# Nine more input chunks held in the first pass's space ahead of a two-layer convolution, and 15 warm-up matmuls in place of 7

## The reference

```
x = x + _L0_conv_ref(_gn(x), L0_conv_w_fft_real, L0_conv_w_fft_imag, ...)
x = x + _L1_conv_ref(_gn(x), L1_conv_weight)
```

## Time and profile before

| | |
|---|---|
| median of 3 runs | 1762.68 us (1761.88 to 1762.94) |
| the profiled execution | 1762.14 us, of which the span is 1760.3 us |
| TensorE matmuls busy | 1653.9 us (94%) |
| VectorE busy | 1381.3 us (78%) |
| ScalarE busy | 1169.0 us (66%) |
| GpSimd busy | 130.9 us (7%) |
| mean granted clock of TensorE | 0.98 |

### The profile page before, as it was taken

One profiled execution on the slowest core, in us unless ns is written; L12 is line 12 of the kernel. 1 busy time (PEld: TensorE's weight loads), 2 busy tenths in 40 slices (PEclk: granted clock), 3 DMA queues, 4 the chain that ended last, 5 costly groups with the idle time before them and its releaser, 6 DMA issues.

```text
span 1760.3 us, 65152 instructions
## 1 busy us (share of the span) xinstructions
PE 1653.9 (94%) x29295; PEld 1263.6 (72%) x29295; DVE 1381.3 (78%) x2202; ACT 1169.0 (66%) x1050; POOL 130.9 (7%) x383
## 2 busy tenths in 40 slices
PE   5888888688799999999999999999999999999999
PEld 5888878554466667887788668866886678666755
DVE  5998999789988888888887888788878888878600
ACT  6888788579666666666666666666666666666444
POOL 0000000032200020002000200020002000100100
PEclk9999899889899999999999999999999999999999
DMA  9999999565456666656665666666666665666245
GB/s 385 421 421 422 422 421 421 210 187 163 121 162 206 199 194 213 216 188 202 214 206 195 202 218 195 205 196 212 196 203 208 202 209 194 209 196 207 110 197 205
DMA packets 101979, 411.65 MB, mean 234 GB/s; under 512 B 17139, under 2 KB 19688, under 8 KB 85352
## 3 DMA queue, kind: packets, MB, share of 16 engines
q1 hardware_dynamic: 100329, 407.51, 65.9%
q10 hardware_dynamic: 735, 0.37, 0.1%
q0 software_dynamic: 672, 0.08, 0.1%
HBM read 271.83 MB, written 136.07 MB: 232 GB/s over the span
## 4 chain that ended last, share of the span: by engine, by line
PE 69%; DVE 16%; issue 8%; ACT 3%; DMA 2%; DVEq 0%; POOL 0%; SPq 0%; ACTq 0%; POOLq 0%
PE ps L459 36%; PE ps L452 32%; DVE x L737 9%; DVE x L957 2%; DVE nat L798 2%; ACT x L578 1%; DVE stats L995 1%; DMA x<-x_pix 1%; ACT x L576 1%; ACT nat L563 1%; DMA x<-wf 1%; PE ps L387 1%; DMA xin<-x_tiles 0%; PE ps L388 0%; DVE x L798 0%
## 5 line engine op out<-in xcount | busy, mean ns | idle before, releaser
L459 PE MATMUL ps<-x,wc 64*64 64x512 f16 (+2 forms) x12585 | 1159.7, 374 | 6.0 <-POOL x L715 6.0
L452 PE MATMUL ps<-nat,wc 64*64 64x512 f16 (+1 forms) x11784 | 1137.6, 377 | 15.3 <-DVE x L957 11.3
L459 PEld LDWEIGHTS ps<-x,wc 64*64 64x64 f16 x12585 | 677.6, 107 | 178.4 <-POOL x L715 7.1
L452 PEld LDWEIGHTS ps<-nat,wc 64*64 64x64 f16 x11784 | 655.9, 107 | 190.2 <-issue 33.3
L563 ACT ACTIVATE nat<-xin,gnp 128x1024 f16<-128x1024 f32 (+1 forms) x249 | 283.3, 1138 | 295.8 <-PE ps L452 284.5
L957 DVE SCALAR_TENSOR_TENSOR x<-ps,gnp,x 128x1024 f16<-128x1024 f32 (+1 forms) x264 | 333.1, 1262 | 31.2 <-ACT x L578 21.6
L593 ACT ACTIVATE outb<-ps,bias 128x1024 f32<-128x1024 f32 (+1 forms) x264 | 289.7, 1097 | 73.1 <-PE ps L459 57.5
L582 ACT ACTIVATE x<-ps,gnp 128x1024 f16<-128x1024 f32 (+1 forms) x229 | 251.0, 1096 | 118.7 <-DVE stats L995 118.4
L798 DVE SCALAR_TENSOR_TENSOR nat<-xin,gnp,nat 128x1024 f16<-128x1024 f32 (+1 forms) x249 | 313.4, 1259 | 2.0 <-ACT nat L563 1.9
L387 PE MATMUL ps<-x 128*128 128x129 f16 x2048 | 259.9, 227 | 54.2 <-DVE x L737 54.0
L737 DVE SCALAR_TENSOR_TENSOR x<-x 128x2048 bf16<-128x2048 f32 x128 | 282.8, 2287 | 19.1 <-DMA x<-wf 17.3
(11 more groups left out here) (139 smaller groups left out, 384.2 us busy)
## 6 DMA issues: line engine op xcount, KB each, us to landing
x<-x_pix SPq DMA_DIRECT2D x128, 1024.0 KB, 11.2
xin<-x_tiles SPq DMA_DIRECT2D x256, 512.0 KB, 3.8
out<-outb SPq DMA_DIRECT2D x256, 512.0 KB, 4.1
xin<-x_tiles SPq DMA_DIRECT2D x8, 192.5 KB, 2.4
out<-outb SPq DMA_DIRECT2D x8, 192.5 KB, 3.0
w<-taps_scratch SPq DMA_DIRECT2D x60, 8.0 KB, 2.9
w<-taps_scratch SPq DMA_DIRECT2D x30, 16.0 KB, 3.2
taps_scratch<-x POOLq DMA_DIRECT2D x21, 3.0 KB, 3.0
```

Of the source, the lines that this page charges most:

```text
L452: return nc.tensor.matmul(ps[64 * kind:64 * kind + 64, bank, 0:w], lhs, planes[rows, xhl, a:a + w], start=first, stop=last)
L459: ins = nc.tensor.matmul(ps[64 * kind:64 * kind + 64, bank, done:done + part], lhs, x1[rows, xhl, z:z + part], start=first and done == 0, ...
```

## The change

Chunks 4 to 12 (`STAGED`) are loaded into `big`, where the first pass had its input, once that pass has read it. They have semaphores of their own. The natural halves of chunks 7 to 12 lie in slots 25 to 30 of `x1`, so 13 chunks have their place at once. The cycle over seven places begins again at chunk 13 (`LAP`), and the change to four places comes at chunk 34 (`TURN`) and not 35. GpSimd makes all pads of image 0, from the scaling factors on (`Z_GNP`); chunks 0 to 12, the join at 4, chunks 13 to 16 and the join at 7 stand ahead of the transfers of the taps of images 1 to 7. ScalarE makes `hi0(0)` between two square roots of the small chain, 1 to 3 ahead of its weight transfers and 4 to 9 behind; in the turns it is ten chunks ahead up to turn 6, makes none in turns 7 to 9 and is seven ahead from turn 10. VectorE makes `lo0(0)` inside the small chain, 1 to 4 ahead of the weights and 5 and 6 behind; in the turns it is seven ahead, as before. 15 warm-up matmuls stand in place of 7.

```diff
-TURN = (NCH // NSEVEN + 1) * NSEVEN
+STAGED = range(NX, NX + 9)
+LAP = STAGED.stop
+TURN = LAP + 3 * NSEVEN
+HI_FIRST = 10
+SIX_AT, STAGE_AT = 25, 6
-WARM = 7
+WARM = 15
+def ahead_hi(g):
+    if g + HI_FIRST < LAP + NX:
+        return g + HI_FIRST
+    return ahead(g) if g + NSEVEN >= LAP + NX else None
...
 def nat_at(g):
-            spot = g % NSEVEN if g < TURN else (g - TURN) % NX
+            if NSEVEN <= g < LAP:
+                return x1, (SIX_AT + g - NSEVEN) * CH
+            spot = g if g < LAP else (g - LAP) % NSEVEN if g < TURN else (g - TURN) % NX
...
+        def x_at(g):
+            if g in STAGED:
+                a = (STAGE_AT + 2 * (g - NX)) * CH // 2
+                return big[:, a:a + CH]
+            return xin[:, g % NX, :]
...
 SyncE:
-                if g >= NX:
-                    sp.wait_ge(lo0_ready, g - NX + 1)
+                if g >= LAP:
+                    sp.wait_ge(lo0_ready, (g % NX if g < LAP + NX else g - NX) + 1)
...
                 sp.dma_start(dst, src).then_inc(late_in, 16)
+            sp.wait_ge(a_lo, B * NACH + ASLOTS)
+            for g in STAGED:
+                load_x(g)
             hold(sp, zve, Z_ZPAD)
...
-            for g in range(NX, 2 * NX):
+            for g in range(LAP, LAP + NX):
                 load_x(g)
...
-                if g + 2 * NX < ALL:
+                if LAP + NX <= g + NSEVEN + NX < TURN + NX:
+                    load_x(g + NSEVEN + NX)
+                if TURN + NX <= g + 2 * NX < ALL:
                     load_x(g + 2 * NX)
...
 ScalarE:
             nc.scalar.activation(zc[0:C, 48:64], zc[0:C, 32:48], ACT.Sqrt).then_inc(zac, 1)
+            hi0(0)
             act.wait_ge(zve, Z_BNVAR)
...
-            for g in range(2):
+            for g in range(1, NX):
                 hi0(g)
             act.wait_ge(zdma, 16 * 4)
             load_weights(act, 0, ((0, 1), (1, 1)), w_in)
-            for g in range(2, NX):
-                hi0(g)
-            for g in range(NX, NSEVEN):
+            for g in range(NX, HI_FIRST):
                 hi0(g)
...
-                if ahead(g) is not None:
-                    hi0(ahead(g))
+                if ahead_hi(g) is not None:
+                    hi0(ahead_hi(g))
...
 GpSimd:
-            pool.wait_ge(zve, Z_TAPS)
-            pool.wait_ge(zdma, 16 * 4)
-            for b in range(1, B):
-                taps_out(pool, b, taps_rest)
+            pool.wait_ge(zve, Z_GNP)
+            for g in range(LAP):
+                first_pad(g)
+            join(NX)
+            for g in range(LAP, LAP + NX):
+                first_pad(g)
+            join(NSEVEN)
+            pool.wait_ge(zve, Z_TAPS)
+            pool.wait_ge(zdma, 16 * 4)
+            for b in range(1, B):
+                taps_out(pool, b, taps_rest)
...
 VectorE:
+            lo0(0)
             after_act(3)
...
-            for g in range(NX):
-                pad(g)
             after_pe()
...
-            for g in range(2):
+            for g in range(1, NX + 1):
                 lo0(g)
             for part in range(4):
                 weights0(0, part)
-            for g in range(2, NX):
+            for g in range(NX + 1, NSEVEN):
                 lo0(g)
-            for g in range(NX, NSEVEN):
-                pad(g)
-            for g in range(NX, NSEVEN):
-                lo0(g)
-            pad(NSEVEN)
```

More of the change, by code:

```diff
@@ L216, in conv_program @@
         x_in = [sem(f"x_in{s}") for s in range(NX)]
+        x_early = [sem(f"x_early{g}") for g in STAGED]
         w_in = sem("w_in")
@@ L534, in _, with hi0 @@
                                              ACT.Identity, scale=AS).then_inc(a_hi, 1)
+            def hi0(g):
+                b, n = divmod(g, NCH)
+                w = CH if n < NFULL else EDGE
+                if g < NCH:
+                    act.wait_ge(pool_pad, g + 1)
+                else:
+                    act.wait_ge(pad_done, g + 1 - NCH)
+                if g >= LAP:
+                    act.wait_ge(pe_done, JOB0[g - (LAP if g < LAP + NSEVEN else NSEVEN if g < TURN + NX else NX)] + 1)
+                planes, a = nat_at(g)
+                nc.scalar.activation(planes[:, 0, a:a + w], x_at(g)[:, 0:w], ACT.Identity,
+                                     scale=gnp[:, 1, b:b + 1]).then_inc(hi0_ready, 1)
             act.wait_ge(zve, Z_VAR)
             nc.scalar.activation(zc[0:C, 48:64], zc[0:C, 32:48], ACT.Sqrt).then_inc(zac, 1)
+            hi0(0)
             act.wait_ge(zve, Z_BNVAR)
@@ L549, in _ @@
                                      bias=trig[:, 2 * k + 1:2 * k + 2], scale=trig[:, 2 * k:2 * k + 1]).then_inc(zac, 1)
[L551 to L564, removed]
             def hi1(g):
@@ L658, in row_ends @@
                     done += w
-            pool.wait_ge(zve, Z_TAPS)
-            pool.wait_ge(zdma, 16 * 4)
-            for b in range(1, B):
-                taps_out(pool, b, taps_rest)
             def first_pad(g):
                 mean = gnp[:, 0, 0:1]
-                slot = xin[:, g % NX, :]
-                pool.wait_ge(x_in[g % NX], 16 * (g // NX + 1))
+                slot = x_at(g)
+                x_landed(pool, g)
                 lo, rows = ROWS_CH * g, ROWS_CH
+                if g == 0:
+                    G.tensor_copy(slot[:, 0:PITCH], mean.to_broadcast([P, PITCH]))
+                    lo, rows = PITCH, ROWS_CH - 1
                 if g == NFULL:
@@ L688, in ends @@
                 column_ends(b, (last + 1) * CH // PITCH if last else 0, TROWS if n == NFULL else (n + 1) * CH // PITCH)
+            pool.wait_ge(zve, Z_GNP)
[9 more added lines that the diff above has]
+                taps_out(pool, b, taps_rest)
             for turn in range(NCH):
-                if DVE_FIRST <= turn + 9 < NCH:
+                if LAP + NX <= turn + 9 < NCH:
                     first_pad(turn + 9)
-                if joins(turn + NSEVEN - 1):
+                if turn + NSEVEN - 1 > NSEVEN and joins(turn + NSEVEN - 1):
                     join(turn + NSEVEN - 1)
```

32 lines of the change are left out of this document (22 added, 10 removed).

## The result

The changed kernel takes 1757.49 us (median of 8 runs, 1755.63 to 1758.74) against 1762.45 us before (8 runs beside them): a ratio of 0.9971, 95% interval 0.9961 to 0.9981. That is 5.0 us or 0.3% faster, by the interval 3.3 to 6.9 us. 1756.2 was forecast with a range of 1753.8 to 1760.3. The profiled execution has a span of 1756.4 us.

What follows compares the result with a forecast made beforehand. TensorE was taken to bound 520 to 1674 us, so an earlier begin of that stage shortens the whole. Gains 4.4 + 0.9 + 1.2 = 6.5 us off 1762.68 gave 1756.2 us, range 1753.8 to 1760.3.

Steps and rivals of the forecast that it cites:

- Part 1: Nine loads after the first pass: landed by 342.5 us, some 6 us of cover before the taps, cost 0.
- Part 2: First high and low parts in the small chain: hi0(0) delays the square root, cost 0.3 us; low parts 0.
- Part 3: 15 warm-ups before the first convolution: they cost nothing and the clock stays at the upper level for the first job.
- Part 4: First turn of image 0: chunk 0's statistics start at 364.5 and not 368.92 us, gain 4.4 us.
- Part 5: Turns 7 to 9 without high parts: VectorE's waits for ScalarE of 0.24 and 0.67 us go, gain 0.9.
- Part 6: Turn-over at 34 instead of 35: one low part leaves the chain before image 0's last mask, gain 1.2 us.
- Part 7: Work moved on GpSimd and SyncE (tap issues, joins, later loads): enough cover, cost 0.
- The lower level in the first job: Rival: clock falls before or just behind the first matmuls; 1757.9 us, or 1759.2 if low all through; chance 0.27.
- Only the start: Rival: only the first turn's 4.4 us is gained, nothing in turns 7 to 9 or the turn-over; 1758.3, chance 0.1.
- Table loads: Rival: hi0(0) in the small chain forces two function table loads, 2.6 us; 1758.8; chance 0.1 with a slow pad.
- Transfers one after another: Rival: the nine loads do not overlap, take 34 us and make the taps 16 us late; 1772 us, chance 0.03.
- A chain made longer by a slow first pad: Rival: GpSimd's first pad takes 1 us longer, small chain +1.1 us; chance 0.1 together with table loads.

Runs made afterwards that it cites:

- e10: e7 with GpSimd's join at chunk 4 moved ahead of the pads of chunks 5 to 12: 1759.69 us, 2.4 below the kernel before.
- e1: The changed kernel with 7 warm-up matmuls in place of 15: 1760.46 us, 1.5 below the kernel before.
- e3: The changed kernel with ScalarE's high parts seven chunks ahead throughout in place of ten at first: 1758.01 us, 4.0 below the kernel before.
- e5: The changed kernel with eight small matmuls ahead of TensorE's wait for GpSimd in images 0 and 7: 1756.46 us, 5.8 below the kernel before.
- e12: The changed kernel with 19 warm-up matmuls in place of 15: 1757.96 us, 4.0 below the kernel before.
- e2: The kernel before with 15 warm-up matmuls in place of 7: 1762.43 us against 1761.97.
- e4: The kernel before with chunk 38's high and low part made in turn 34, not 31: 1761.56 us against 1761.97.
- e6: The changed kernel with chunk 0's high and low part behind the small chain: 1757.73 us, 4.5 below the kernel before.
- e7: The changed kernel with the nine loads behind the weights' transfers and low part 4 behind the weights: 1762.26 us against 1762.27 before.
- e8: The changed kernel with the edits of e5 and e6 together: 1756.32 us (5 runs), 6.0 below the kernel before.

## Why the prediction was right

**Part 1, the loads: 0 was right.** The ninth load was in at 345.0 and not at 342.5, which used 2.5 of the 6 us of cover; the taps left no later for it. e10 shows what the early time buys beyond the space: 2.4 us, together with the place of low part 4.

**Part 2, the small chain: 0.3 was taken, about right in size, and by luck.** T to C is 31.73 to 31.96 in the six profiles with the changed kernel's order up to C (the changed kernel twice, e1, e3, e5, e12) and 31.75, 31.30 and 31.55 with the order of before (before, e2, e4). But the term that was reckoned, `hi0(0)` ahead of the square root, is not there: it was over before the root's data were, and the row of L591 shows 0.17 us of idle time, released by VectorE. Two other things cost. One operation of VectorE took 0.36 us in place of 0.18 as GpSimd's pads began. It takes 0.35 or 0.36 in all eleven profiles with these pads (also in e6, which has the pads and not the first parts in the chain), where the root starts 15.78 to 15.83 behind T, and 0.18 in the three without, where it starts at 15.61 or 15.62. So the pads are the likely cause, though no run moved them alone. And low part 4, put at "0, with hardly any room", held the weights up: VectorE no longer waits for the taps. In e7 and e10, with low part 4 behind the weights and the loads late, C comes about 0.9 us earlier.

**Part 3, the warm-ups: right.** VectorE's first mask was forecast 4.75 us behind C and came 4.78 behind it. The level was up at the first job in each of the six profiles of kernels with 15 warm-ups and early loads (the changed kernel twice, e3, e5, e6, e8), with waits for the weights from 0.85 to 1.79 us. The page of the Trainium skill ("TensorE: Matmul & The Clock Gate", "What's actually happening") would let the level fall only after a longer idle stretch. The first job agrees with it, the last stage does not: there a wait of 2.46 us, shorter than the 3.97 in the earlier trace rows, let it fall in nine executions of eleven.

**Part 4, the first turn: 4.4 forecast, 4.5 measured.** T to S is 37.54 against 42.02. e1 and e2 show that it takes both halves. But the execution before that all these rows came from was a late one at this place: e4, which has the same order up to S, took 41.02, and e2 41.30. The mean of the three is 41.4, and that of the five profiles with the changed order, early loads and 15 or more warm-ups 37.4 (37.54, 37.37, e3 37.38, e5 37.34, e12 37.32): the gain is 4.1. The forecast hit the pair because both sides of it came from the same late execution.

**Part 5, turns 7 to 9: 0.9 forecast, 0.6 measured in its place** (the mask of turn 10 is 29.17 behind S, 29.79 before, and 29.83 in e3), of which 0.5 are left at the last mask (1.63 - 1.11). The mechanism was right and the term too large. The idle time shown beside an instruction (0.24 and 0.67) is not all a wait for the other engine: between the end of the mask and the lo1 some 0.15 us are idle even where nothing is waited for (388.60 to 388.75 in the changed kernel), and 0.24 + 0.67 less twice that is 0.6.

**Part 6, the turn-over: 1.2 forecast; 1.1 by the profile of the changed kernel** (VectorE's lead grew from 4.77 us at the mask of turn 31 to 5.88 at the last mask) and by that of e4 between the same marks.

**Part 7: 0, right.** The 21 issues ran from 367.90 to 380.5, and the next join came at 385.87.

**The sum.** 6.5 was forecast up to the last mask and 6.1 was there in the profiles. The medians say 5.0 and 4.8. With several executions of either order at the start, the parts are 4.1 + 0.5 + 1.1 = 5.7 and not 6.1. So 0.8 of the 1.5 to 1.7 us that the forecast was too high are explained: two terms were mis-sized, part 4 by 0.3, since a single execution's start was taken as the kernel's, and part 5 by 0.4, mostly since idle time was taken as wait; part 6 gives the last 0.1. The 0.7 to 0.9 us between 5.7 and the medians lie inside the intervals and remain open. The fall in the last stage could hold some of it: it is in both profiles of the changed kernel and in two of three with the old order (e2, e4, not before), too few to say that one meets it more often. The time lies in the range, and the mechanisms of parts 3 to 6 are shown; how near the total came says little, since the interval of the gain is itself 3.6 us wide.

**The rivals.** The lower level in the first job: not seen with 15 warm-ups, and e1 shows its price, 3.7 in the profile where 3.0 (4.4 - 1.4) was forecast for the worst case. That sum was wrong: its 366.4 is the end of a first job in which the clock rose at 364.6. By its own figures a job at the lower level all through ends at 358.95 + 21 x 0.43 + 0.2 = 368.2, which leaves no gain at all; in e1 the level rose in the last part of the job. For the milder case, 3.4 us of the job at the lower level, no row of before shows such a stretch, and no run met it. Only the start: refuted by S to M. Table loads: none. Transfers one after another: the nine were in within 15.6 us of the first issue, not 34. A chain made longer by a slow first pad: not seen either; what stands against the pads is the 0.2 of part 2. The upper end of the range has the late pad's 1.1 on top of the 0.3 that it should replace; by its own figures it is 1760.0, and nothing hangs on it.

## What to carry to other kernels

Warm-up matmuls pay only where TensorE is what the next step waits for: here they were worth nothing that could be told with late input and 3.3 to 3.7 us with early input, and the rest of the change 1.5 us without them. When loads are moved, look at what stands behind their consumers in each engine's list: one copy behind eight pads was worth 2.4 us. When work is put ahead of something that waits for a transfer, look at how long that wait was at its shortest: two more low parts filled a wait of 2.74 us and overran it a little. For differences of a few microseconds cut several profiles of both kernels at the same marks, and compare stage by stage; a single execution of before stood 0.6 us off the mean of three at the start.

## What was not expected of the hardware

A wait of 2.46 us on TensorE, amid dense matmuls at a granted clock of 1.00, was followed by a fall to 0.5 in nine profiles of eleven, and cost 1.67 us; with a wait of 0.48 us it never was in three. In e2 the first job ran at 1.00 behind a gap of 1.79 us. Seven warm-ups brought the level up in one profile of three: in that of before it rose near their end and fell again, in e1 and e4 it stayed at 0.50 through them and into the first job. From the last mask of image 0 to that of image 7, with the same work, executions took 1188.3 to 1188.6 us in three profiles (before, changed, e10) and 1187.4 to 1187.9 in the other eleven. And an operation of VectorE on 128x24 elements with two inputs in SBUF took 0.36 us where it had taken 0.18, when copies of GpSimd began beside it.
